# Second bank's job behind the transposed scores, loads and key products at other places

## The reference

```python
x = x + xcond0(layernorm(x), ctx, ctx, tau, delta, ...)
x = x + ffn0(layernorm(x), ...)
x = x + xcond1(layernorm(x), ctx, ctx, tau, delta, ...)
x = x + ffn1(layernorm(x), ...)

# xcond, 16 heads of 16 channels
scores = einsum('blhe,bshe->bhls', q @ Wq.T + bq, k @ Wk.T + bk)
scores = scores * tau[b] + delta[b, s]
a = softmax(scores / 4)                       # over the 375 keys
out = einsum('bhls,bshd->blhd', a, v @ Wv.T + bv) @ Wo.T + bo
```

## Time and profile before

| What | Value |
|---|---|
| median of three runs | 1386.84 us |
| profiled execution | 1388.7 us, of which the traced span is 1386.7 us |
| busy in the span: PE, DVE, ACT, POOL | 1228.9 us (89%), 852.7 (61%), 500.3 (36%), 484.9 (35%) |
| mean granted clock of PE | 0.918 of full speed |
| opening of layer 0 | 0 to 47 us |
| 16 bodies of layer 0 | 47 to 373 us: PE busy 310.32 of 326 us, clock 0.97 |
| tail of layer 0 | 373 to 441 us: 50.05 of 68 us, clock 0.73 |
| experts of layer 0 | 441 to 653 us: 208.44 of 212 us |
| shared products, opening of layer 1 | 653 to 714 us: 33.93 of 61 us, clock 0.84 |
| bodies of layer 1 | 714 to 1087 us: 337.87 of 373 us, clock 0.90 |
| tail of layer 1 | 1087 to 1124 us: 16.06 of 37 us, clock 0.50 |
| experts of layer 1, end | 1124 to 1387 us |

### The profile page before, as it was taken

How to read it: one execution, slowest core, us unless ns; L and a number is a source line. 1 busy time by engine, 2 the same in 40 slices (tenths; PEclk the granted TensorE clock), 3 DMA queues, 4 the chain that set the end, 5 groups by cost and what they waited for, 6 DMA issues and landing times. The chain is left out here.

```text
span 1386.7 us, 39900 instructions
## 1 busy us (share of the span) xinstructions
PE 1228.9 (89%) x12642; PEld 951.1 (69%) x12643; DVE 852.7 (61%) x2710; ACT 500.3 (36%) x1238; POOL 484.9 (35%) x646
## 2 busy tenths in 40 slices
PE   4899999999877999998839998999999669999995
PEld 2566666666545899897426666666666459999995
DVE  2358877887766666665465767676775444444442
ACT  1355455554321444443114544444444212222221
POOL 0114455455363001100545555555522213333332
PEclk8699999999768999999958999998999579999998
DMA  7233444444334678864222433333322413333423
GB/s 190 72 104 120 139 128 136 142 126 134 106 107 160 194 213 259 262 176 145 67 70 79 103 80 97 82 91 91 87 60 74 157 30 89 110 102 105 141 46 80
DMA packets 112457, 164.77 MB, mean 119 GB/s; under 512 B 26272, under 2 KB 93312, under 8 KB 111216
## 3 DMA queue, kind: packets, MB, share of 16 engines
q0 software_dynamic: 22672, 58.41, 16.5%
q1 hardware_dynamic: 48880, 59.42, 14.8%
q10 hardware_dynamic: 40832, 46.05, 10.1%
HBM read 87.82 MB, written 61.64 MB: 108 GB/s over the span
## 5 line engine op out<-in xcount | busy, mean ns | idle before, releaser
L986 DVE TENSOR_REDUCE mx<-banks 112x2 f32<-112x750 f32 x256 | 235.3, 935 | 77.5 <-PE banks L610 75.3
L1713 POOL DMA_INDIRECT xs_d<-xns,idx x160 | 155.5, 972 | 189.4 <-PE banks L632 148.5
L1455 ACT ACTIVATE shared_buf<-banks 125x672 f32<-125x672 f32 x256 | 173.1, 728 | 73.0 <-PE banks L632 72.7
L865 PEld LDWEIGHTS banks<-xT,attn_buf 128*128 128x128 f32 x1408 | 163.8, 194 | 4.7 <-DVE xT L1343 3.1
L865 PE MATMUL banks<-xT,attn_buf 128*128 128x128 f32 x1408 | 164.3, 277 | 2.5 <-DVE xT L1343 2.5
L1724 POOL DMA_INDIRECT kept<-y_d,yidx x128 | 126.5, 988 | 85.5 <-PE banks L632 48.8
L813 PE MATMUL banks<-xT,staged 128*128 128x128 f32 x1064 | 142.5, 277 | 6.7 <-DVE staged L1354 6.6
L632 PE MATMUL banks<-attn_buf 18*125 18x112 f32 x3072 | 129.3, 301 | 14.5 <-DVE mx L986 12.2
L813 PEld LDWEIGHTS banks<-xT,staged 128*128 128x128 f32 x1064 | 130.8, 194 | 7.7 <-DVE xT L1343 7.3
L632 PEld LDWEIGHTS banks<-attn_buf 18*125 18x125 f32 x3072 | 105.4, 200 | 44.0 <-DVE mx L986 22.5
L610 PE MATMUL banks<-attn_buf 17*112 17x375 f32 x1024 | 119.4, 537 | 7.9 <-DVE mx L986 5.6
(11 more groups left out here) (205 smaller groups left out, 1873.0 us busy)
## 6 DMA issues: line engine op xcount, KB each, us to landing
shared_buf<-xs_d SPq DMA_DIRECT2D x136, 128.0 KB, 2.6
y_d<-shared_buf ACTq DMA_DIRECT2D x132, 128.0 KB, 2.6
ringbuf<-in_we SPq DMA_DIRECT2D x6, 2176.0 KB, 8.5
ringbuf<-in_we POOLq DMA_DIRECT2D x32, 384.0 KB, 4.8
attn_buf<-attn_buf SPq DMA_DIRECT2D x128, 93.8 KB
attn_buf<-in_ctxT ACTq DMA_DIRECT2D x26, 375.0 KB
xs_d<-zrow ACTq DMA_DIRECT2D x16, 512.0 KB, 3.1
y_d<-zrow ACTq DMA_DIRECT2D x16, 512.0 KB, 4.5
```

The costliest lines, as they stand in the source:

```text
L865: last = pe.matmul(dst, staged[:, u % 2, k * 2 * L.I + c * P:k * 2 * L.I + (c + 1) * P], xT[:, u % 2, k, :], start=(k == 0), stop=(k == KD ...
L986: dve.tensor_reduce(mx[:, i % 2, 2 * p:2 * p + 2], banks[0:Q, 2 * p:2 * p + 2, 0:S], AX.X, ALU.max).then_inc(s_max, 1)
L1455: act.activation(pT[:, slot:slot + 2, :], banks[0:KT, first_bank:first_bank + 2, 0:ST * Q], ACT.Exp, scale=0.25).then_inc(s_exp, 1)
L1713: pool.indirect_dma_start(xs_d[L.number], bass.IndirectOffsetOnAxis(ap=idx[:, b % 2, k:k + 1], axis=0), rows, None).then_inc(s_scat[b % 2] ...
```

## The change

**Bodies.** The list BEFORE is called BEYOND, and its job runs on PE behind `scores_T`, ahead of the two BEHIND jobs of the same quarter. On ACT its copy goes between the two exp instructions of the quarter. On DVE the moments of the residual that OP has made become a job of their own (MOM2), from quarter 1 to the start of quarter 2, and SLOT goes to quarter 3. In layer 1, C0 and C1 of batch b + 4 come into quarter 3, C2 and C3 of batch b + 3 stand in quarter 0, MOM goes to quarter 1 and LN1 to quarter 2. POOL's gathers follow.

**Opening of layer 0.** The weights wo, rw, bo and ebias, the rest of x, and the weights of the shared expert and of layer 1 are issued from ACT's queue, behind the copies of Q(0), K1(1) and Q(1), in this order. On PE the first score rows and maxima run before XT, Q of batch 1 and the bias rows.

**Tail of layer 0.** V2 and V01 of batch 0 and K0 and K1 of batch 1, all of layer 1, are computed between the router and the table rows. The tables leave banks 6 and 7 for banks 2 and 3 (3 and 4 in layer 1), and the shared products of group 1 run behind them.

**Experts of layer 0.** Three output rows stand in the unrolled tiles, thirteen in the first thirteen turns of the tile loop (a turn has four tiles), and the last batch's R4, W80 and W81 follow these turns.

**Opening of layer 1.** It has no output rows and no V and K jobs. The last shared product (DOWN3) runs behind XT and Q of batch 0; the first maxima run between the combines of batch 1.

```diff
-        BEFORE = (("XT", 2), ("O2T", -1), ("RK", -2), ("V2", 1))
+        BEYOND = (("XT", 2), ("O2T", -1), ("RK", -2), ("V2", 1))
...
-        FIRST_JOBS = ((("K0", 0), ("V2", 0), ("K1", 0), ("XT", 0), ("V01", 0), ("Q", 0), ("K0", 1), ("XT", 1), ("K1", 1), ("Q", 1)),
-                      (("XT", 0), ("Q", 0), ("V2", 0), ("V01", 0), ("K0", 1), ("K1", 1), ("BO", 0), ("ROWS", 0), ("MAX", 0), ("XT", 1), ("Q", 1)))
+        FIRST_JOBS = ((("K0", 0), ("V2", 0), ("K1", 0), ("XT", 0), ("Q", 0), ("V01", 0), ("K0", 1), ("K1", 1), ("ROWS", 0), ("MAX", 0), ("XT", 1), ("Q", 1), ("BO", 0)),
+                      (("XT", 0), ("Q", 0), ("DOWN3", 0), ("ROWS", 0), ("MAX", 0), ("XT", 1), ("Q", 1), ("BO", 0)))
...
-            load(s_wts[0], 0, "wo", "rw", "bo")
-            sp.dma_start(resid[:, 3:B, :], a["x"][:, 3:B, :]).then_inc(s_wts[0], 16)
...
                     for i in range(NQ):
...
-                        j, r = BEFORE[i]
-                        if in_layer(b, r):
-                            job(j, n + r, (u + r) % 2, free[1])
...
                         scores_T(n, u, i, b)
+                        j, r = BEYOND[i]
+                        if in_layer(b, r):
+                            job(j, n + r, (u + r) % 2, free[1])
...
                     job("RK", n, 1, [(ev["LG"], n + 1)])
                     if l == 0:
-                        shared_down(0)
-                        shared_up(1)
+                        shared_up(0, 1)
+                        job("V2", n + 1, 0, [(ev["RK"], n + 1)], l=1)
+                        job("V01", n + 1, 0, [(ev["K1"], n + 2)], l=1)
+                        job("K0", n + 2, 1, [(ev["V01"], n + 2)], l=1)
+                        job("K1", n + 2, 1, [(ev["K0"], n + 3)], l=1)
+                        shared_down(0, {2: (ev["K1"], n + 3), 3: (ev["V2"], n + 2)})
                     table_rows()
...
-                    WORK = ((("MAX", 0), ("C0", 3), ("R1", -2), ("C1", 3), ("OT", -1)),
-                            (("R2", -2), ("MAX", 0), ("C2", 3), ("OP", -1)),
-                            (("RK", -2), ("MAX", 0), ("LN2", -1), ("C3", 3), ("MOM", 3), ("SLOT", -2)),
-                            (("R3", -2), ("MAX", 0), ("LN1", 3), ("W80", -2), ("W81", -2), ("R0", -1)))
+                    WORK = ((("MAX", 0), ("C2", 3), ("R1", -2), ("C3", 3), ("OT", -1)),
+                            (("R2", -2), ("MAX", 0), ("MOM", 3), ("OP", -1)),
+                            (("MOM2", -1), ("RK", -2), ("MAX", 0), ("LN2", -1), ("LN1", 3)),
+                            (("SLOT", -2), ("MAX", 0), ("R3", -2), ("C0", 4), ("W80", -2), ("W81", -2), ("C1", 4), ("R0", -1)))
...
-                with dve.Fori(0, L.turns) as i:
...
+                with dve.Fori(0, B - ROWS_AHEAD) as i:
+                    turn(i)
+                    start(i + SP_ROWS)
+                    output_rows(i + ROWS_AHEAD)
+                    close()
+                start(SP_LAST)
+                weights_of_last()
...
+                def rest_in():
+                    weights_in(act, s_wts[0], 0, "wo", "rw", "bo")
+                    act.dma_start(ebias[:, :], a["ebias"].partition_broadcast(Q)).then_inc(s_wts[0], 16)
+
+                def x_in():
+                    act.dma_start(resid[:, 3:B, :], a["x"][:, 3:B, :]).then_inc(s_wts[0], 16)
...
+                LOADS_BEHIND = {("Q", 0): rest_in, ("K1", 1): x_in, ("Q", 1): layer1_in}
...
-                        j, r = BEFORE[i]
-                        if j in OWN and in_layer(b, r):
-                            job(j, n + r, b + r, (u + r) % 2)
...
                         exp(n, i, 0)
+                        j, r = BEYOND[i]
+                        if j in OWN and in_layer(b, r):
+                            job(j, n + r, b + r, (u + r) % 2)
...
                         exp(n, i, 1)
```

More of the change, by code:

```diff
@@ L676, in first @@
                             free[m] = [(ev[j], n + (r + 1))]
-                    if l == 0:
-                        pe.wait_ge(s_wts[l], REST_IN[l])
-                        for sm, v in free[1]:
-                            wait(pe, sm, v)
-                        bias_rows()
-                        score_rows(n, 0, 0)
-                        score_rows(n, 0, 1)
-                        max_T(n, 0, free[0])
                 def body(n, b, u):
                     free = [[(s_mev, n * NQ + 1)], [(ev["LG"], n - 1)]]
-                    if l and not in_layer(b, -1):
+                    if not in_layer(b, -1):
                         free[0].append((ev["Q"], n + 2))
@@ L696, in body @@
                     if not in_layer(b, -1):
[L697 removed]
+                        free[1] = [(s_bo2, l + 1)]
                     elif not in_layer(b, -2):
@@ L789, in shared @@
                 pe.wait_ge(s_tiles, 1)
-                for i in range(2, 4):
-                    shared_up(i)
-                    shared_down(i)
+                for m in range(KD):
+                    shared_up(2, m)
+                shared_down(2)
+                for m in range(KD):
+                    shared_up(3, m)
             def xt(l, t, u, dst):
@@ L1141, in first @@
                             row_max(base, i, p)
-                    close()
                 def first1():
@@ L1211, in last @@
                         table_in()
+                        start(SP_LATE)
+                        shared_rows(0)
                         shared_products(1)
-                        start(SP_LATE)
-                        shared_rows(0, (2, 3))
-                        for j in (weights, "W80", "W81"):
-                            extra(j, n, b, 1)
-                        shared_rows(1)
                         close()
@@ L1574, in last @@
                         shared_silu(0)
+                        for j, r in (("V2", 0), ("V01", 0), ("K0", 1), ("K1", 1)):
+                            job(j, n + 1 + r, r, r, l=1)
+                    act.wait_ge(s_tabm, 2 * l + 1)
+                    act.activation(tabr[0:1, 0:2, :].rearrange("o k t -> o (k t)"), bank[TABLE_BANK[l]][0:1, :], ACT.Copy).then_inc(s_tabi, 1)
+                    if l == 0:
                         shared_silu(1)
-                    act.wait_ge(s_tabm, 2 * l + 1)
-                    act.activation(tabr[0:1, 0:2, :].rearrange("o k t -> o (k t)"), bank[6][0:1, :], ACT.Copy).then_inc(s_tabi, 1)
                 bodies(act, L, body, first, last, 2, 4)
```

275 lines of the change are left out of this document (162 added, 113 removed), and 2 rows, old and new, of the table WORK.

## The result

The changed kernel takes 1500.42 us, the median of four runs (1495.10 to 1506.23), the kernel before 1386.70 us. The ratio is 1.082 (95% interval 1.080 to 1.084), +114 us where +44 was predicted. The profiled execution took 1503.0 us (span 1501.3).

The account below looks back on a forecast made before the run. Attention bodies were taken as bound by PE's own queue plus its idle. Terms 31 + 26 (bodies) - 8 - 1 + 9 - 13 (openings, tail, experts) gave +44 us, forecast 1431 us, own range 1415 to 1447, wider range 1384 to 1460.

Parts of the forecast that it names:

- Idles of a body: Attention bodies: new PE waits less those gone, +2.2 us a body, +31 us in layer 0 and +26 in layer 1.
- the 0.77 us that the working took off: Layer 1 bodies: DVE's wait for score rows at a body's start, subtracted to get DVE 1.1 us late.
- a body's change counts about 28 times: Attention bodies: with 16 bodies a layer, a body's change counts about 28 times, the openings once each.
- The clock: Attention bodies: only idles change; in layer 1 today's clock loss, 1.66 us of busy time a body, was left as is.
- The first rival: Layer 0 bodies: the clock falls there too, 14 by 1.66, +23 us, 1454 us; chance 0.18.
- The second rival: Layer 1 bodies: DVE not late and the clock holds; 12 bodies give 0 in place of 26, 1405 us; chance 0.22.
- the Trainium skill's rule on the clock: TensorE: the clock falls only after idle longer than any in these bodies; the prediction noted it fell after 1.37 us.
- Experts of layer 0: Tile loop: thirteen output rows at 0.5 us each plus 2.5 for the last batch's weights, +9 us (bounds 3 and 15).
- Openings and tail: Opening of layer 0 -8 us (-10 to -4), of layer 1 -13 (-20 to -6), tail of layer 0 -1 (-4 to +3).
- as the prediction feared: Opening of layer 0: PE's bias rows wait for the 1456 KB of x, landing 10.2 us after issue before the change.
- The 3 us that the working allowed for slowed row copies: Opening of layer 0: layer 1's 2 MB of loads would slow the first body's row copies, some 3 of the 8 us.
- The third rival: Openings win 10 + 20 us, more than bodies lose, if a body costs under 0.9 us: 1382 us; chance 0.16.

Follow-up runs that it names:

- e_fill2: The changed kernel with fewer identity products than e_fill in PE's idle times (one ahead of the maximum's transpose in three quarters, four before Q, three before XT2): 1439.6 us.
- e_rows: The changed kernel with the output rows back in the unrolled tiles of layer 0's experts and in layer 1's opening: 1538.1 us, ratio 1.074.
- e_undo: The changed kernel with the second bank's jobs back ahead of the transposed scores, on PE and ACT, the rest kept: 1467.1 us, ratio 1.024.
- e_before: The kernel before, unchanged, measured again on occasion 2 on another chip: 1435.4 us, ratio 0.997.
- e_fill: The changed kernel with identity products in every body: two ahead of each maximum's transpose, six before Q, four before XT2: 1507.8 us, ratio 1.052.
- e_bfill: The kernel before with three identity products ahead of o's transposes in quarter 1 of layer 1's bodies: 1375.6 us, ratio 0.992.

## Why the prediction was wrong, point by point

- **Idles of a body: right.** L631 mostly 0.31 to 0.42 us (0.40 predicted) but up to 1.04 once a body in about half of them, Q 0.92 (0.94), XT2 0.65 (0.60), DVE late in layer 1 and PE's idle there up to 2.06 (1.5), since the 0.77 us that the working took off were not to be had. In sum +27.6 us in layer 0 and +23.0 in layer 1, for 31 and 26. (The working says that a body's change counts about 28 times; its sum rightly uses 14 + 12.)
- **The clock: the step that failed.** The working said "The PE instructions stay the same; only the idles change." and, for layer 1, "so I leave that loss as it is". In fact the new idles brought the clock down in layer 0, where it had held, and kept it down for longer in layer 1: +25.3 and +42.3 us of busy time, 68 us in place of 0. The first rival had the mechanism and nearly the price for layer 0 (23 us) at a chance of 0.18; it had no term for layer 1, where the loss of 1.66 us a body grew by 42.3 / 12 = 3.5. e_fill2 shows the cause: the same waits with work in them, on the same occasion, cost 68 us less.
- **The second rival** (DVE not late, the clock holds in layer 1) did not come: the maxima there were late by more than predicted, and the clock was 0.80.
- **Why the working could miss it.** I compared single idles with the 1.17 us that had not cost the clock and the 1.37 that had the earlier trace rows. The trace of before doesn't bear that out as a bound. Its timeline of PE in two later bodies, o's transposes and the V products behind them (1.99 us at the upper level):

```profile
988.34 0.38 PE L539 MATMUL banks<-con,o 112*128 112x112 f32 x2 [1.38 <-DVE o L994]
...
990.37 1.99 PE L544 MATMUL banks<-wv,attn_buf 128*125 128x256 f32 x8
...
1010.44 0.38 PE L539 MATMUL banks<-con,o 112*128 112x112 f32 x2 [1.29 <-DVE o L994]
...
1012.99 3.09 PE L544 MATMUL banks<-wv,attn_buf 128*125 128x256 f32 x8
```

1.38 us cost nothing there, 1.29 did, and the earlier trace rows show 0.35 and 1.03 ahead of V products of 3.64 us. The changed body has five or six idles with 2.6 to 3.3 us in all. The sentence on the Trainium skill's rule on the clock (TensorE: Matmul & The Clock Gate, HAM oscillation) stands as it did: the trace disagrees, here with the clock lost after 0.42 and 0.93 us.
- **Experts of layer 0: right in sign, half in size.** I took 0.5 us a row from the unrolled tiles; a row in a turn cost 1.03 to 1.24 us, nearly its whole 1.18 us on DVE. The last batch's weights cost near the predicted 2.5 (2.89 in e_rows), and the products behind that idle ran at the lower level (2.05 us for 1.06).
- **Openings and tail: right.** -5.3, -12.6 and -3.1 us, each within its bounds. In layer 0 PE waited 3.42 us for the rest of x ahead of its bias rows, as the prediction feared, and the first transposed scores ran at 42.06 (39 predicted). The 3 us that the working allowed for slowed row copies were not told apart by any run.
- **The third rival** (openings win, bodies cost under 0.9 us) gave the openings 30 us; they won 18, and its condition did not come.
- Still open: what decides in which bodies of layer 0 the clock falls (last section), and what layer 1's order on DVE costs in the changed kernel itself on the same occasion; a move with bank 7 freed ahead of the combines wasn't tried.

## What to carry to other kernels

Where TensorE runs at full clock with little idle, price a new wait twice: its own length, and what the same products cost when the clock falls behind it. Do not compare a new idle with the longest that did no harm. Their sum doesn't foretell the loss either: e_undo's layer 1 had 26 us of idle and a clock of 0.79, e_before's, on another occasion, 37 us and 0.88. Read the clock from the duration of one repeated product, and try the new waits filled. Filling an unavoidable wait with harmless products was worth 68 us here and 10 in the kernel before (19 in the stage itself). It won nothing in layer 0 of e_fill, where the products were longer than the waits and waited themselves. A job that covers a reduction's latency isn't free to move, however little it takes.

## What the runs showed of the hardware

- The length of the last waits alone does not decide whether the clock falls. At 238.86 and 241.05 idles of 0.85 and 0.92 us did not lower it, at 262.02 and 264.21 idles of 0.42 and 0.93 did. The first body had begun at the lower level (its V products took 2.93 us for eight, at 221.09), the second at the upper, and from 170 to 323 us bodies of near 24.8 and 26.2 us take turns. But the next body, which also begins at the lower level (3.06 us), loses the clock again, so where a body begins doesn't decide it either. What does was not tested.
- One product of f32 with a 128 by 128 weight and 112 columns is two instructions for TensorE. At the upper level three in a row took 0.92 us (e_bfill), four 1.06 (e_fill2), six 1.50 (e_fill).
- The kernel before took 1436 us on occasion 1 and 1386 on occasion 3, on one and the same chip, and 1437 on occasion 2 on another. The profile of e_before is from occasion 2. In it the excess is in the bodies (354 and 390 us for 340 and 364) and the tail of layer 0 (61 for 54). Of it 25 us are longer busy time in the bodies, at a granted clock of 0.93 and 0.88 for 0.95 and 0.91. Another part is PE's wait for maxima, as the totals of PE's waits show, in the first profile of before:

```profile
PE banks L539 <- DVE o L994: 25.1, 26, 1.4
PE banks L632 <- DVE mx L986: 12.2, 34, 0.8
```

and in e_before:

```profile
PE banks L632 <- DVE mx L986: 24.3, 49, 1.5
PE banks L539 <- issue: 14.0, 12, 1.4
PE banks L539 <- DVE o L994: 10.6, 14, 1.4
```

A row has the engine and the instruction that waits, what it waits for, the us in total, the number of waits and the longest. The waits before the transposed scores doubled. Those that the profile ends with "issue" are no excess: with the waits for o they are 24.6 us, as the 25.1 before. Why the maxima came later on that occasion was not found.
